# Four transformer layers on one core: streams in opposite phase, and attention outputs written transposed in strips

## The reference, cut to what matters

```
layer 0: q = x Wq, k = ctx Wk * mask * 2/DH, v = ctx Wv; per token, a softmax over 16 x 16
         (feature by feature, summed over the heads); x = LN(Wo(out)); x = LN(x + relu(x W1 + b1) W2 + b2)
layer 1: x += att8(LN(x), LN(x)); x += att8(LN(x), ctx); a, g = LN(x) W1 + b1; x += (a * gelu(g)) W2 + b2
layer 2: x = LN(x + att(x, x, mask)); x = LN(x + att(x, ctx, pad mask)); x = LN(x + relu(x W1 + b1) W2 + b2)
layer 3: x += att(LN(x), ctx); x += att(LN(x), LN(x), mask); x += gelu(LN(x) W1 + b1) W2 + b2

att:  softmax(q k^T / 4 + mask) v, per head, then the output product Wo
att8: the same with q, k, v and the softmax weights rounded to 8 bits (clipped)
```

## Time and profile before

| | |
|---|---|
| median of 3 runs | 2274.02 us |
| the profiled execution | 2274.92 us |
| its span | 2273.2 us |
| mean granted TensorE clock | 0.899 |
| TensorE busy | 1921.8 us (85%) |
| VectorE busy | 1307.1 us (57%) |
| GpSimd busy | 996.9 us (44%) |
| ScalarE busy | 967.8 us (43%) |
| bytes moved | 34.88 MB, 15 GB/s |

### The profile page before, as it was taken

One profiled execution on the slowest core, in us unless ns is written; L12 is line 12 of the kernel. 1 busy time (PEld: TensorE's weight loads), 2 busy tenths in 40 slices (PEclk: granted clock), 3 DMA queues, 4 the chain that ended last, 5 costly groups with the idle time before them and its releaser, 6 DMA issues.

```text
span 2273.2 us, 32499 instructions
## 1 busy us (share of the span) xinstructions
PE 1921.8 (85%) x10497; PEld 1507.4 (66%) x10497; DVE 1307.1 (57%) x2218; ACT 967.8 (43%) x2274; POOL 996.9 (44%) x1235
## 2 busy tenths in 40 slices
PE   4666667677887887887999899998988999999997
PEld 3565556454664655664777677777766787787776
DVE  5877778658558558658444465454533635436361
ACT  1111221224334333334546465564644665556563
POOL 5566665535335336345333454434533423333330
PEclk8889998677877887887999999999988999999999
DMA  7100000000200000000000200000000000000000
GB/s 216 69 5 5 9 5 5 5 1 6 79 1 5 5 0 5 5 0 5 6 1 6 79 0 9 0 5 5 1 5 5 6 6 0 5 23 0 9 1 10
DMA packets 31292, 34.88 MB, mean 15 GB/s; under 512 B 3196, under 2 KB 30040, under 8 KB 30808
## 3 DMA queue, kind: packets, MB, share of 16 engines
q1 hardware_dynamic: 31192, 33.70, 4.8%
HBM read 31.60 MB, written 2.10 MB: 15 GB/s over the span
## 4 chain that ended last, share of the span: by engine, by line
PE 60%; DVE 11%; issue 4%; POOL 2%; ACT 2%; DVEq 0%; POOLq 0%; ACTq 0%
PE ps L503 31%; PE ps L670 9%; PE ps L701 8%; PE ps L680 6%; PE ps L514 3%; DVE xn L874 2%; DVE rowmax L1010 1%; DVE rowsum L1016 1%; PE ps L696 1%; PE ps L668 1%; DVE work L1012 1%; DVE work L1004 1%; DVE O L845 1%; POOL x_all L1126 1%; DVE stats L864 0%
## 5 line engine op out<-in xcount | busy, mean ns | idle before, releaser
L503 PE MATMUL ps<-hT,w_slot 128*128 128x256 f32 x1856 | 455.1, 399 | 21.1 <-ACT hT L744 21.1
L503 PEld LDWEIGHTS ps<-hT,w_slot 128*128 128x128 f32 x1856 | 359.7, 199 | 77.8 <-ACT hT L744 24.0
L1190 POOL TENSOR_TENSOR work<-KT,own_head 128x512 f32<-128x512 f32 x256 | 261.5, 1047 | 288.6 <-ACT KT L756 234.3
L680 PEld LDWEIGHTS ps<-ident,work 128*128 128x128 f32 x1536 | 206.4, 154 | 178.3 <-issue 110.6
L670 PE MATMUL ps<-work,QT 128*128 128x512 f32 x512 | 276.5, 622 | 22.8 <-POOL work L1190 20.6
L680 PE MATMUL ps<-ident,work 128*128 128x128 f32 x1536 | 265.5, 301 | 35.6 <-POOL work L1199 35.6
L1199 POOL TENSOR_SCALAR work<-work,winv 128x128 f32<-128x128 f32 x512 | 184.9, 384 | 218.9 <-DVE winv L1029 218.4
L886 DVE TENSOR_TENSOR x_all<-ps,x_all 128x512 f32 (+1 forms) x88 | 60.7, 690 | 379.6 <-PE ps L503 326.9
L829 ACT ACTIVATE work<-work,rowmax 128x128 f32<-128x128 f32 x768 | 245.0, 392 | 68.1 <-DVE rowmax L1008 66.5
L701 PEld LDWEIGHTS ps<-V,work 128*128 128x128 f32 x2048 | 251.2, 192 | 7.4 <-issue 4.4
L701 PE MATMUL ps<-V,work 128*128 128x17 f32 x2048 | 248.9, 254 | 2.4 <-ACT work L818 2.4
(11 more groups left out here) (119 smaller groups left out, 3015.6 us busy)
## 6 DMA issues: line engine op xcount, KB each, us to landing
ctx_in<-in_ctx SPq DMA_DIRECT2D x32, 256.0 KB, 2.7
w_slot<-in_L_xattn_W SPq DMA_DIRECT2D x2, 1024.0 KB, 6.4
w_slot<-in_L_xattn_ff_w SPq DMA_DIRECT2D x1, 2048.0 KB, 11.2
w_slot<-in_L_xattn_ffn_w SPq DMA_DIRECT2D x2, 1024.0 KB, 9.9
w_slot<-in_L_xattn_w SPq DMA_DIRECT2D x2, 1024.0 KB, 9.3
out<-x_all SPq DMA_DIRECT2D x8, 256.0 KB, 2.1
x_all<-in_x SPq DMA_DIRECT2D x1, 1536.0 KB, 11.7
pad<-in_mask_Bx1x1xS_fk SPq DMA_DIRECT2D x1, 1024.0 KB, 6.7
```

The lines of the kernel that those rows point to most:

```text
L503: mm = pe.matmul(dst, lhsT(k), rhs(k), start=(k == 0), stop=(k == chunks - 1))
L680: mm = pe.transpose(bank(2 + u % 2)[:, tok(h)], prob[u % NP][:, tok(h)], ident[:, :])
L1190: pool.tensor_tensor(KB[u % NK].rearrange("p (h k) -> p h k", h=HU), keys, own_head[:, half * HU:(half + 1) * HU].unsqueeze(2).broadcast_t ...
```

## The change

1. **Halves.** `one_pass` no longer alternates attentions. `half` runs both attentions of one stream with its short chain between them, and the other stream's long chain beside all of it, its slots multiplied by a factor (`stretched`) so that it lasts as long.
2. **A bank for the short chain.** Its products, transposes and residual use bank 5 (`third`) alone, whichever of `one` and `other` they had, so `q` waits for the evacuation of `k`, and `v` for that of `q`. Attention outputs of both sequences go to bank 4 (`o_bank`).
3. **Strips in plain attention.** Layers 2 and 3 use the zero-padded V as the weight (128x32) and write transposed strips. The column of ones is gone: VectorE sums each unit (`row_sums`), takes all reciprocals, and spreads each over the 16 features of its head; four transposes on TensorE and a ScalarE copy bring them into the layout of the output (`inverse_rows`, `inv_T`), and one VectorE product per attention scales the output. `ot` is left out in layers 2 and 3.
4. **Feed-forward pieces** stand half a slot apart, and `y2` is emitted in four parts (half of the hidden size for one sequence each).
5. V of the quantised layer shares the buffer of the plain one, which is set to zero again at the start of layer 2. Semaphore counts follow the new order.

```diff
 def pieces_of(kind, arg):
     if kind == "out":
-        return [("ot", 1), ("y", 0), ("sum", 1)]
+        return [("y", 0), ("sum", 1)] if "direct" in arg else [("ot", 1), ("y", 0), ("sum", 1)]
     if kind == "ffn":
         n = FC if arg["act"] == "geglu" else FC // 2
-        return [(f"f{f}", (f % 2 == 2 - 1) + 0 * (f == n - 1)) for f in range(n)] + [("y2", 0), ("sum", 1)]
+        return [(f"f{f}", 0.5) for f in range(n)] + [(f"y2{n}", 0.5) for n in range(Y2)] + [("sum", 1)]
...
-    y2 = spot_of["y2"]
+    y2 = spot_of["y20"]
     if "stage" in kinds:
-        at = {"ctx": spot_of["y"] + 2, "stage": y2 - 4}
+        at = {"ctx": spot_of["y"] + 2, "stage": y2 - 2}
     elif STEPS[layer][-1][0] == "ffn":
-        at = {"ctx": spot_of["y"] + 2, "norm": y2 - 4, "scale": y2 - 3}
+        at = {"ctx": spot_of["y"] + 2, "norm": y2 - 2, "scale": y2 - 1}
...
+    y2 += Y2 // 2
...
+def stretched(pieces, slots):
+    factor = max(1.0, slots / (max(p[0] for p in pieces) + 1))
+    return [(int(p[0] * factor),) + p[1:] for p in pieces]
...
+            def half(layer, g, st, pieces):
+                mix_at, at, mine = {}, 0, []
+                for m in range(len(PLAN[layer]) // 2):
+                    if m:
+                        between = chain(layer, g, st, m, True)
+                        mine += [(at + int(p[0]),) + p[1:] for p in between]
+                        at = max(p[0] for p in mine)
+                    kind, arg, n = PLAN[layer][2 * m + 1]
+                    step = emit_mix(kind, layer, g, st, arg, n, m)
+                    for i in range(STEPS_OF[kind]):
+                        mix_at[at + i] = partial(step, i)
+                    at += STEPS_OF[kind]
+                together(mix_at, mine + stretched(pieces, at - 1), late)

             def one_pass(layer, g, after):
                 n_mix = len(PLAN[layer]) // 2
-                for m in range(n_mix):
-                    if m:
-                        attend(layer, g, 0, m, chain(layer, g, 1, m))
-                    attend(layer, g, 1, m, joined(layer, g, after, 0) if m == n_mix - 1 and after else chain(layer, g, 0, m + 1))
+                half(layer, g, 1, joined(layer, g, after, 0) if after else chain(layer, g, 0, n_mix))
                 if after:
-                    attend(*after, 0, 0, joined(layer, g, after, 1))
+                    half(*after, 0, joined(layer, g, after, 1))
...
                 def values(u):
...
-                        for h in range(HU):
-                            hh = u % UJ * HU + h
-                            mm = pe.matmul(bank(4 + j)[:, hh * width:(hh + 1) * width], PT[u % 2][:, tok(h)], V[st][:, j, hh, :],
-                                           start=True, stop=True)
+                    out_u = o_bank[:, m * T + j * S:m * T + (j + 1) * S]
+                    for n in range(0 if quant else 2, 4):
+                        for x in range(2):
+                            pair, e = u % UJ * 2 + x, n % 2
+                            at = pair % 4 * 32
+                            lhsT = (Vzb if quant else Vz)[st][:, j, pair, 2 * e:2 * e + 2, :]
+                            rhs = below[:, :].broadcast_to([P, S]) if n < 2 else (PTb if quant else PT)[u % 2][:, tok(2 * x + e)]
+                            mm = pe.matmul(out_u[at:at + 32, :], lhsT, rhs, start=(n == (0 if quant else 2)), stop=(n == 3))
...
+                def row_sums(u):
+                    dve.wait_ge(s["exp_ready"], U * ap + u + 1)
+                    dve.tensor_reduce(rowsums[:, u * HU:(u + 1) * HU], prob[u % NP].rearrange("p (h k) -> p h k", h=HU), AX.X, ALU.add)\
+                        .then_inc(s["nsums_ready"], 1)
+                def all_inverses():
+                    dve.reciprocal(oinv[:, :, :], rowsums.rearrange("p (g h) -> p g h", g=G)).then_inc(s["oinv_ready"], 1)
+                    inv = oinv[:, :, :].unsqueeze(3).broadcast_to([P, G, H, DH])
+                        dve.tensor_copy(inv_cols[:, :, :, :], inv).then_inc(s["inv_cols_ready"], 1)
                 def outputs():
                     dve.wait_ge(s["o_ps"], U * (ap + 1))
...
+                    dve.wait_ge(s["inv_T_ready"], np_ + 1)
+                    dve.tensor_tensor(OT[st].rearrange("p c t -> p (c t)"), o_bank, inv_T, ALU.mult).then_inc(s["o_ready"], G)
```

More of the change, by code:

```diff
@@ L3 @@
 from contextlib import ExitStack
+from functools import partial
 FP32 = mybir.dt.float32
@@ L153, with together @@
 AFTER = ("norm", "scale")
[L156 to L166 removed]
+def together(mix_at, pieces, late):
+    slots = max([p[0] for p in pieces] + list(mix_at)) + 1 + late
+    for i in range(slots):
+        if i in mix_at and not late:
+            mix_at[i]()
+        for slot, emit, piece, arg, n in pieces:
+            if slot == i - (late if piece != "ot" else 0) and not (late and piece in AFTER):
                 emit(piece, arg, n)
[L168 to L171 removed]
+        if i in mix_at and late:
+            mix_at[i]()
+        for slot, emit, piece, arg, n in pieces:
+            if slot == i - late and late and piece in AFTER:
                 emit(piece, arg, n)
+def stretched(pieces, slots):
+    factor = max(1.0, slots / (max(p[0] for p in pieces) + 1))
+    return [(int(p[0] * factor),) + p[1:] for p in pieces]
 def layer_weights():
@@ L364, in passes, with chain @@
         def passes(eng, emit_mix, emit_piece, late, before_last=lambda layer: None):
-            def chain(layer, g, st, number):
-                return [(spot, emit_piece(layer, g, st), piece, arg, n) for piece, spot, arg, n in PLAN[layer][2 * number]]
+            def chain(layer, g, st, number, aside=False):
+                return [(spot, emit_piece(layer, g, st, aside), piece, arg, n) for piece, spot, arg, n in PLAN[layer][2 * number]]
             def joined(layer, g, after, st):
-                return join(layer, after[0], emit_piece(layer, g, st), emit_piece(*after, st))
@@ L388, in one_pass @@
                 else:
-                    together(None, 0, chain(layer, g, 1, n_mix), late)
-            together(None, 0, chain(0, 0, 0, 0), late)
-            attend(0, 0, 0, 0, chain(0, 0, 1, 0))
+                    together({}, stretched(chain(layer, g, 1, n_mix), 0), late)
+            together({}, stretched(chain(0, 0, 0, 0), 0), late)
+            half(0, 0, 0, chain(0, 0, 1, 0))
             for layer in range(NL):
@@ L504, in product, with emit_piece @@
                 return mm
-            def emit_piece(layer, g, st):
+            def emit_piece(layer, g, st, aside):
                 q = c[st]
                 w = weight[layer]
+                left, right = (third, third) if aside else (one, other)
                 def turned(dst, src):
@@ L644, in emit_mix @@
                 mp = phase("mix", layer, g, mix, st)
[L645 removed]
                 lag = ATT_LAG[quant]
+                np_ = None if quant else phase("natt", layer, g, mix, st)
                 def scores(u):
@@ L711, in step @@
                         values(i - lag - 1)
+                    if not quant and i == INVERSE_AT:
+                        inverse_rows()
                 return step
@@ L770, in emit @@
                         act.activation(V0[st], other.rearrange("p (g h d) -> p g h d", g=G, h=H), ACT.Copy).then_inc(q["locV_ready"], 1)
-                    elif piece == "ot" and "direct" not in arg:
+                    elif piece == "ot":
                         act.wait_ge(q["ot_ps"], use("turned", layer, g, n["turned"]) + 1)
@@ L1057, in step @@
                         inverses((i - SUM_LAG) // 2)
-                    u = i - lag - 1
-                    if 0 <= u < U and u % UJ == UJ - 1:
-                        outputs(u // UJ)
+                    if not quant and 0 <= i - SUMS_AT < U:
+                        row_sums(i - SUMS_AT)
+                        if i - SUMS_AT == U - 1:
+                            all_inverses()
+                    if i == U + 4:
+                        outputs()
                 return step
```

162 lines of the change are left out of this document (80 added, 82 removed), and 2 rows, old and new, of the table STEPS.

## The result

The changed kernel takes 2337.1 us (median of 4 runs) beside 2274.3 for the kernel before on the same chip: ratio 1.0276, 95% interval 1.0258 to 1.0293. It is 63 us slower, where 93 us faster was forecast. The profiled execution took 2335.1, its span is 2333.4.

A forecast was written before the change was run, and what follows sets the result against it. The prediction took TensorE as the bound, with VectorE pacing layer 0 and neither full in layer 1. Terms of -45, -24, -12, -15 and +3 sum to -93 us, giving 2181 us, range 2095 to 2265.

The forecast's parts named there:

- Step (1): Plain attention's value products: fp32 strips overlap in pairs, gaining 0.10 us per unit, 26 us over 256 units.
- A: Rival for the plain value products: fp32 strips do not overlap, giving 2262 us; chance 17%.
- E: Rival for the plain value products: all four heads of a unit run at once, giving 2097 us; chance 2%.
- Step (2): Row sums in plain attention: 173 us more on VectorE fits under 130 per pass; the attention's end gets shorter.
- Step (3): Order of a half: dense products lie where no attention step is, hiding the own chain; about 0.5 us exposed twice in layer 1.
- Step (4): Sum by layer: layer 1 -45, layer 2 -24, layer 3 -12, change from layer 2 to 3 -15, layer 0 +3 us.
- Layer 1: Quantised layer: a half takes 81 us against 86.6, -45 us over eight halves.
- Layer 2: Layer with masked first attention: a half takes 68.5 us against 71.5, -24 us in all.
- Layer 3: Layer with unmasked first attention: TensorE stays the bound, a half takes 65.3 us against 66.85, -12 us in all.
- C: Rival in a half's middle: own chain exposed, with three products through one bank, giving 2337 us; chance 8%.
- B: Rival in layers 2 and 3: VectorE becomes the bound of every masked attention, giving 2253 us; chance 11%.
- D: Rival in layer 2's first attentions: TensorE's granted clock falls, some 15 us in each of eight halves, giving 2301 us; chance 4%.

The follow-up runs named there:

- e6: Changed kernel's strips in the old order, with VectorE's row sums cut to 8 constant elements per head (softmax not normalised): 2265.4 us, ratio 0.9969.
- e8: Changed kernel's strips in the old order, complete, with row sums accumulated by ScalarE with the exponentials instead of by VectorE: 2268.1 us, ratio 0.9983.
- e5: Changed kernel (new order) with VectorE's row sums cut to 8 constant elements per head, so the softmax is not normalised: 2337.9 us, ratio 1.0284.
- e9: Changed kernel with GpSimd weighing only one of four heads per unit in layer 1, the rest left out: 2306.6 us, ratio 1.0144.
- e2: Changed kernel with the short chain's q and v in banks of their own instead of one shared bank: 2333.2 us, ratio 1.0269.
- e4: Changed kernel with the long chain's pieces emitted ahead of the short chain's in a shared slot: 2375.7 us, ratio 1.0460.
- e3: Changed kernel with row sums one step earlier, and inverses and the first attention's output scaling two steps earlier: 2318.9 us, ratio 1.0208.
- e12: e8 with, in layer 2, GpSimd's last post-scaling of stream 0's long chain issued behind the next attention's first spread of keys: 2260.7 us, ratio 0.9944.
- e1: Changed kernel put back to the old order, piece distances and short-chain banks, keeping strips and VectorE's row sums: 2309.1 us, ratio 1.0163.
- e11: Changed kernel with the feed-forward chain's hidden products spread evenly from about slot 6 through the first attention: 2445.2 us, ratio 1.0744.

## Why the prediction was wrong, step by step

**What bounds the kernel: right.** Layer 3 was TensorE's work, and what spoiled it was anything that put TensorE in a wait.

**Step (1), strips: right, with the gain a little small.** 0.13 us a unit instead of 0.10. The fp32 strips overlap in pairs: eight passes take 0.56 us to the next operation. That is what the Trainium skill (TensorEngine Tiling (Array Packing), Key Properties) says of different tiles, and the trace agrees. Rivals A and E are out. The 33 us of 256 units did not reach the end even in the old order: e6 is 8 us faster than the kernel before, e8 6. In e6 TensorE waits 46.5 us for the norm in layers 2 and 3 (24.1 and 22.4) against 27.6 before (12.3 and 15.3), and 9.1 us with "issue" as the reason: 28 us, about what is missing.

**Step (2), row sums: right in the sum, wrong in two clauses.** They fit in the new order (e5: no gain without them). But "what gets shorter is the end of an attention" is wrong: TensorE waits up to 1.5 us for OT after each of 12 attentions in three passes of layer 3, 13.0 in all, and only 1.4 us in all before. The steps for sums and inverses come after the last unit, and behind them stands no product; I took one VectorE operation for the path and left out the inverses that must come before it. And "it fits under 130" holds for the busy time alone: in the old order the same work, in the same totals, costs 44 us through the norms queued behind it.

**Step (3), order: the step that failed.** I wrote that the dense products lie "exactly where no attention step is" and read it as good. The own chain is hidden, as I said (TensorE 20.31 of 20.8 us busy in the middle), but I never asked what then covers the 13 steps of attention on either side. Only a few q, k, v and output products of 8 passes each lie there. The sum took the attentions at the pace of the busiest engine; the runs show the waits of a unit's path through four engines (spread, scores, maximum, exponentials, transposes, copy, values) instead: at every few units in layer 1, and in layer 3 at the first units and behind the last one, while the units between do run at TensorE's 2.06 us. Without the sums on VectorE this order costs 72 us (e5 against e6).

**Step (4), the terms.**
- Layer 1: -45 forecast, +19 measured. A steady half is 87.2 us, not 81. In the half shown the first attention takes 27.6 us (25 to 26 with its tail), the middle 25.6 (20 to 21, and TensorE was truly busy for 24.2 of it, so its work was counted too small), the second 32.5 (35 to 36). I paced a quantised unit by VectorE's three operations; GpSimd's four of 0.38 us, in series with them, were not in the sum, and e9 puts 31 us on three of them. The two "issue" waits of 3.8 and 3.9 us were in no term either.
- Layer 2: -24 forecast, +1. Waits were put at 4.1 us a half (3 and 1.1) and are (13.7 + 10.4 + 6.3 + 6.1 + 3.0)/6 = 6.6. The 3.4 us wait for GpSimd's spread did go.
- Layer 3: -12 forecast, +33. 0.9 us of waits a half were planned, 37.2/6 = 6.2 came: 64.4 + 6.2 = 70.6, and 425.9/6 = 71.0 was measured.
- Layer 2 to 3: -15 forecast, about 0. The two stalls for the norm are 4.0 us instead of 8.8, as the row below shows, but the two stretches around them take 55.1 + 51.2 us against 53.1 + 53.6.
- Layer 0: +3 (0 to +8) forecast, +7.

TensorE in order of time, changed kernel, at the change from layer 2 to 3:

```profile
1688.44 0.63 PE L537 MATMUL ps<-ident,xn 128*128 128x128 f32 x4 [4.01 <-DVE xn L913]
```

**The rivals.** C named 2337 us, which is what was measured, and that is a coincidence. Its mechanism was an exposed own chain and three products in one bank; the middle is full, and separate banks give 4 us (e2). What it had right is the sign, and that the own chain is close to TensorE's path: TensorE waits 1.0 us a half for its V in layer 3, and what e4 puts ahead of it costs 39 us. B is excluded by e5, D by the clock of 1.00 in the pass of layer 2 shown above. The rival that was missing is "both attentions bare", and the stretch table had its price: the stretch in layer 1 where an attention ran without dense products had TensorE at 13.39 of 19.4 us and the clock at 0.67.

Open: which of the small waits of layer 3 that e3 leaves (half of its loss) gives what, since no run takes them singly; the 7 us of layer 0, where nothing was tried; and that e12's layer 3 shows no gain. There TensorE waits twice, 4.3 and 4.4 us, before a score product with "issue" as the reason (up to 5.1 us in e1, above), which the kernel before does not show in that layer. These waits, and the two of layer 1 in the changed kernel, stand at the first scores of the second and the third trip of the loop over a layer's passes. Their cause was not tried.

## What to carry to other kernels

In this case dense work of another stream was a supply of cover: before moving it to one stretch, write down for every stretch of the new order what TensorE does between two steps of the latency-bound work, and price the uncovered ones with the worst such stretch of the present trace. Busy shares of an engine (VectorE "95 of 130") don't say what its work costs; what stands behind it in the same queue does, and here the same sums cost 44 us in one order and none in the other. Test the parts of a change in all combinations: getting the sums off VectorE was worth nothing in the changed kernel, and 41 of the 48 us between e1 and e12 in the old order. The combination left out here, new order with old value products, is the one that would part the order from the strips' way out.

## What was not expected of the hardware

- Reading ScalarE's accumulated sum is a separate instruction of 192 ns (where the exponential reads `work`) to 240 ns (where it reads PSUM) behind each exponential of 393 to 399 ns.
- Eight fp32 passes on two strips, two per head back to back, took 0.56 us to the next operation; the prediction's sum for no overlap was 8 x 0.11 + 0.09 = 0.97.
- What the clock can cost behind an attention: in e11, behind a first attention with TensorE 84% busy and a last wait of 1.70 us, eight passes of 256 columns took 3.49 us at a granted clock of 0.54, where they take 1.89 us at full clock. In the changed kernel's steady layer 3 the first eight passes behind the first attention took 3.5 to 3.6 us in two of six halves and 1.99 us in the other four, behind the same wait of 1.51 us each time; no run here shows what parts the two.
